# Graph layer on one core: 60 of 196 edge blocks selected by one-hots, and five steps ahead of the loop

## The reference, cut to what matters

```python
msg = concatenate([x[dst], x[src] - x[dst]])    # 64 wide
h = relu(msg @ W1 + b1)                         # 64
h = relu(h @ W2 + b2)                           # 128
h = relu(h @ W3 + b3)                           # 64
m = h @ W4 + b4                                 # 32
s = segment_sum(m, dst) / max(count(dst), 1)
out = layernorm(x + s)
```

## Time and profile before

| | us |
|---|---|
| timed runs, median of 3 | 1566.78 |
| timed runs, lowest and highest | 1564.91, 1569.15 |
| profiled execution: its own time, from first to last instruction (the span) | 2441.1 |
| PE busy in the profile | 1767.5 |
| POOL busy in the profile | 1125.9 |
| DVE busy in the profile | 947.9 |
| ACT busy in the profile | 602.6 |

### The profile page before, as it was taken

One profiled execution on the slowest core, in us unless ns is written; L12 is line 12 of the kernel. 1 busy time (PEld: TensorE's weight loads), 2 busy tenths in 40 slices (PEclk: granted clock), 3 DMA queues, 4 the chain that ended last, 5 costly groups with the idle time before them and its releaser, 6 DMA issues.

```text
span 2441.1 us, 39243 instructions
## 1 busy us (share of the span) xinstructions
PE 1767.5 (72%) x13131; PEld 1040.0 (43%) x13131; DVE 947.9 (39%) x3086; ACT 602.6 (25%) x945; POOL 1125.9 (46%) x1165
## 2 busy tenths in 40 slices
PE   3133777777768777878787778786867778777797
PEld 2112444444444444444444444444444444444454
DVE  3663343333333343333333333443333333333356
ACT  2233122222212222212222222222221222122234
POOL 5275444453544454354545454544444454444411
PEclk7555787877878787777778877777877877787888
DMA  5334643343434443353434353544344344444332
GB/s 128 98 93 88 200 112 112 106 140 94 136 101 116 126 121 109 103 147 91 135 105 136 104 152 92 152 109 114 104 123 115 111 114 109 133 118 118 109 106 59
DMA packets 189929, 283.06 MB, mean 116 GB/s; under 512 B 84614, under 2 KB 90169, under 8 KB 189156
## 3 DMA queue, kind: packets, MB, share of 16 engines
q1 hardware_dynamic: 152341, 241.67, 33.7%
q0 software_dynamic: 36704, 37.00, 7.3%
q10 hardware_dynamic: 682, 1.85, 0.3%
HBM read 266.51 MB, written 13.73 MB: 115 GB/s over the span
## 4 chain that ended last, share of the span: by engine, by line
PE 63%; issue 23%; another core or an unknown queue 6%; DVE 3%; ACT 2%; DMA 1%; SPq 1%; DVEq 0%; POOL 0%; ACTq 0%; POOLq 0%
PE ps L964 22%; PE ps L996 12%; PE ps L988 10%; PE ps L1019 5%; PE ps L1004 4%; PE ps L919 3%; PE ps L901 3%; PE ps L1016 2%; PE ps L978 2%; ACT work L716 1%; ACT work L731 1%; DMA sums<-in_src 1%; DVE region L1410 0%; DVE region L1292 0%
## 5 line engine op out<-in xcount | busy, mean ns | idle before, releaser
L585 POOL DMA_INDIRECT xj<-z_rows,src_t x1107 | 1074.5, 971 | 1190.9 <-PE ps L919 787.7
L964 PE MATMUL ps<-region,x_p 128*96 128x150 bf16 (+53 forms) x5876 | 569.6, 243 | 416.6 <-issue 407.2
L964 PEld LDWEIGHTS ps<-region,x_p 128*96 128x96 bf16 x5876 | 440.6, 142 | 572.9 <-issue 566.7
L731 ACT ACTIVATE work<-ps,b3s 128x512 f32<-128x512 f32 x196 | 134.7, 687 | 1335.5 <-PE ps L996 1037.1
L996 PE MATMUL ps<-work,w3s 128*64 128x512 f32 x784 | 356.6, 840 | 21.2 <-issue 21.1
L1377 DVE TENSOR_SCALAR region<-region,cst 128x1565 bf16<-128x1565 int16 (+6 forms) x416 | 245.7, 634 | 268.0 <-remote 256.3
L988 PE MATMUL ps<-work,w2s 64*128 64x512 f32 x784 | 298.1, 827 | 6.8 <-ACT work L716 5.6
L724 ACT ACTIVATE work<-ps,b2s 128x512 f32<-128x512 f32 x392 | 250.7, 684 | 161.0 <-PE ps L988 82.7
L1392 DVE COPY work<-ps 128x512 f32<-128x512 f32 x194 | 133.4, 687 | 336.4 <-PE ps L1004 217.0
L1386 DVE CAST work<-ps 96x512 bf16<-96x512 f32 x52 | 35.7, 686 | 513.9 <-PE ps L964 506.8
L1410 DVE TENSOR_SCALAR region<-iota_g,dst_rel 128x42 f32<-128x42 f32 x1120 | 185.7, 250 | 0.0
(11 more groups left out here) (156 smaller groups left out, 826.3 us busy)
## 6 DMA issues: line engine op xcount, KB each, us to landing
dstb<-dst_rows SPq DMA_DIRECT2D x196, 252.0 KB
region<-src_rows SPq DMA_DIRECT2D x104, 391.2 KB
region<-src_rows SPq DMA_DIRECT2D x52, 407.2 KB
region<-src_rows SPq DMA_DIRECT2D x52, 403.2 KB
region<-src_rows SPq DMA_DIRECT2D x52, 376.2 KB
region<-src_rows SPq DMA_DIRECT2D x52, 375.8 KB
region<-src_rows SPq DMA_DIRECT2D x52, 374.0 KB
region<-src_rows SPq DMA_DIRECT2D x52, 366.2 KB
```

The costliest lines, as they stand in the source:

```text
L585: pool.indirect_dma_start(out=xj[:, u, j % UT, j // UT, 0:w], out_offset=None, in_=rows, in_offset=bass.IndirectOffsetOnAxis(ap=cols[:, j: ...
L964: chosen = nc.tensor.matmul(ps[0:XP, XBANK[h], lo - h * UE:hi - h * UE], xb[:, a, :], hot[:, q % QN, at + lo:at + hi], start=not begun[h], ...
```

## The change

`SB` goes from 52 to 60 and `AHEAD` from 4 to 5. The steps at which decode, the casts and the store of the sorted dst rows stand had been written relative to `AHEAD`; they now have names with the numbers 2 and 3 that they had. The first sorted block moves from step 7 to step 9. With the larger `SB`, the 59 spacings between sorted blocks become three steps (57 times) and four (twice), where 23 of the 51 were three and 28 four; the gathered blocks fall from 144 to 136, the gathers from 1147 to 1083, and `LP`, half of the gathered blocks, from 72 to 68.

```diff
-SB = 52
+SB = 60
 HALVES = 64
 GB = S_N - SB
 B0 = SB * PE2
...
-AHEAD = 4
-HALF_STEP, PARTS_STEP = 0, 1
-FIRST_SORTED, LAST_SORTED = AHEAD + 3, S_N - 8
+AHEAD = 5
+HALF_STEP, PARTS_STEP, DECODE_STEP, CAST_STEP = 0, 1, 2, 3
+FIRST_SORTED, LAST_SORTED = AHEAD + 4, S_N - 8
 SORTED_AT = [FIRST_SORTED + k * (LAST_SORTED - FIRST_SORTED) // (SB - 1) for k in range(SB)]
...
             for s in range(AHEAD):
-                if s == AHEAD - 1:
+                if s == CAST_STEP:
                     sp.wait_ge(s_cast, 1)
...
-                if s == AHEAD - 1:
+                if s == CAST_STEP:
                     act.wait_ge(s_rowi, 1)
...
-                if s == AHEAD - 2:
+                if s == DECODE_STEP:
                     decode()
```

## The result

The changed kernel takes 1574.76 us (median of 7 runs, 1572.13 to 1575.65) against 1567.42 us for the kernel before in the same runs: 1.0046 times as long, interval 1.0033 to 1.0059. It was forecast at 1498. The time lies in the wide range of 1465 to 1600 (not in the forecast's own, 1475 to 1550), but the sign is wrong: a small loss, clear of noise, where a gain of 4% was expected.

What follows compares the result with a forecast made beforehand. The prediction took GpSimd (POOL) and its gathers as the bound of the timed loop. It summed 1567 - 81 + 5 - 3 + 10 = 1498 us, with its own range 1475 to 1550 and a wide range 1465 to 1600.

Steps and rivals of the forecast that it cites:

- PE's clean pace: TensorE's undisturbed loop time: 4.50 us per gathered block and 11.25 per sorted one, 1215 us for the old loop.
- POOL as the bound: GpSimd's gathers bound the timed loop: 1107 at 1.25 to 1.276 us, 1503 to 1532 us with both ends.
- leftover 35 to 64 us: Timed 1567 us above GpSimd's sum, taken as GpSimd's own waits, such as 14.89 us before the loop opens.
- item 1: Eight gathered blocks become sorted: 64 gathers fewer take 81 us off GpSimd; TensorE gets 54 us more beside it.
- Item 5: Nearer spacing of sorted blocks: periods of 20.25 us on TensorE, 20.4 on GpSimd; 10 us added for waits, 0 to 60.
- rule of the Trainium skill: GpSimd can't write gather descriptors during fast two-port VectorE operations; at its hardest +41 us, giving 1539.
- Rival A: TensorE is already last in the timed loop, so the change slows it to about 1624 us; chance 0.21.
- Rival B: Near spacing costs TensorE 1.2 us a period more, 70 us, eating the gain: 1567 us; chance 0.14.
- Rival C: More GpSimd waits vanish because TensorE's holding of the ring in near spacings ends: 1460 to 1475 us; chance 0.06.
- item 3: Sort stages keep their steps; two more gathered steps before the first selection hide first window loads: gain 3 us, 0 to 15.
- item 2: One more step ahead of the loop delays its opening, where GpSimd waits: 5 us added, ends 0 and 7.
- span that was to rise by 50 to 90 us: Profiled execution, taken as TensorE-bound: the 49.5 us TensorE gains in work should lengthen its span by 50 to 90 us.

Runs made afterwards that it cites:

- the second trace: The kernel before, unedited, profiled once more without being held up by the profile: 1565.21 us, beside 1564.69 for the same kernel; trace span 1563.4.
- the short one-hots: Changed kernel with source-number one-hots made for a quarter of their columns from the sixth sorted block on: 1463.08 us, 0.9348 of before.
- the gaps behind one-hots: Changed kernel in which VectorE waits for each source-number one-hot to finish before its next instruction: 1512.98 us, 0.9653 of before.
- the one gap: Changed kernel in which VectorE waits for the adding of the sums before a step's first source one-hot: 1463.43 us, 0.9338 of before.

## Why the prediction was wrong, point by point

*PE's clean pace* was right: 11.25 + 2 x 4.50 = 20.25 us for a period of three is what the changed kernel shows while gathers last. *POOL as the bound* was right, with the first gather from z_rows at 78 and the end 43 to 45 us after the last. The leftover 35 to 64 us over POOL's sum were no wait before the loop opens, since POOL waits for nothing there: some 30 us of it was excess, 1107 x (0.998 - 0.971). The disturbed trace's mean of 0.971 came from an execution in which POOL waited for PE for a third of the span, and VectorE was busy for 39% of it, against 60% in the second trace; that these are why the gathers looked cheap there is not shown.

*The step that failed* is item 1 of the parts: "64 x 1.25 = 80 us, x 1.276 = 82 us off POOL; I take 81, since both ends are near". The count was right. The price of the remaining 1043 was held at what the trace had shown, as if it did not depend on the change; it rose from 1.303 to 1.390 us with the 0.305 between them, 1043 x 0.087 = 91 us. What the runs showed in its place: the nearer spacing makes 55 places where VectorE's unbroken run holds a gather, and one wait that breaks the run there brings the price down to 0.969 us and the time to 1463. Item 5 had the periods (nobody in them is idle), but booked 10 us, with 0 and 60 as ends, for waits that neither side makes up; it was no wait but the length of POOL's own gathers, and 88.

*The rule of the Trainium skill* ("SBUF — State Buffer", "SBUF: two separate sides", the box "The DVE blocks DMA trap") was the one that spoke against the change, and I gave it no chance of its own. Its direction is borne out by the short one-hots (1463 us), the gaps behind one-hots (1513) and the one gap (1463); its worst case as I worked it out (64 more one-hots at 0.634 us, 41 us) was half of what came. It counted the 64 added one-hots, each at its own length; but at the 55 places a gather waits for all three one-hots, those that were there before too, and loses 1.7 us in the mean. Elsewhere the trace agrees with the rule one instruction at a time: a gather is let in when the one-hot that it met has ended.

*Rival A* (PE last already, 1624) is refuted by the second trace of before. *Rival B* came nearest in time (1567), by another mechanism: PE lost nothing in the near periods until it waited for gathers. *Rival C* did not come. The sentence on the range is wrong in one thing: A's sum, 1567 + 54 to 63 us, lies above 1600 altogether, not with its upper end alone. The entry gain of item 3 would have been PE's, which was not last. The 5 us of item 2 came out about in size (4 to 6), but not by a wait of POOL's before the loop, which has none. The span that was to rise by 50 to 90 us can't be judged: the later executions were not held up by the profile as the first was.

## What to carry to other kernels

A count times a price holds only if the price doesn't depend on what else changes: when two engines become evenly loaded, ask for what the one could hold the other up, and look at the longest instances of the priced instruction, not at its mean. Two engines that each repeat a period can lock, so that the one meets the other's worst place every time; a jump in a mean that no single long wait explains is then found in the order of time, by looking for equal distances, and by asking what the other engine's program has at that place and nowhere else. Before an engine's work is cut to free another, try a wait of some tens of nanoseconds in its chain: here one wait was worth 111 us.

## What the runs showed of the hardware

- An indirect DMA of 128 rows takes GpSimd 0.944 us, and the next follows 0.305 us later, in all 13 undisturbed traces; those that no VectorE instruction overlaps take 0.94 to 0.96 us, the longer ones stand beside VectorE.
- The large bf16 one-hots (L1377, and L1369 for destinations) hold a gather; it ends 0.81 or 0.12 us after the end of a one-hot. Small fp32 one-hots and additions hold none by themselves (0.948 us in the mean of 110).
- Mostly a gather is let in at the end of one large one-hot, even when the next follows without a gap (1.25 us in the rows above). Behind an unbroken run of 3 us, three of them hold it to the end of the third: 2.0 to 2.7 us, at 55 of 55 places of the changed kernel. A gap of 35 ns ahead of the first ends that. By what port, and why the run ahead matters, the runs do not tell.
- The first profiled execution of the kernel before was 874 us longer than the timed runs; the other 13 profiles of this program and its variants lie within 5 us of theirs. Why is open.
